# z of jobs 1 to 3 made by VectorE from PSUM in a routed expert layer

## What is computed

```python
expert_ids = jnp.minimum(tid // (25000 // 4), 3)
for e in range(4):
    g = silu(einsum('bsd,fd->bsf', layernorm(x), ctx[e]))
    u = einsum('bsd,fd->bsf', layernorm(x), ctx[e])
    y = einsum('bsf,df->bsd', g * u, ctx[e])
    out = where(expert_ids == e, y, out)
x = x + tanh(g_xattn) * out
x = x + tanh(g_ffn) * fp8_linear(layernorm(x), weight)
```

## Time and profile before

| what | value |
|---|---|
| time, median of 3 runs | 197.42 us (197.24 to 197.56) |
| the profiled execution's own time | 197.25 us |
| its span in the trace | 195.5 us, so 1.75 us lie around it |
| busy: PE, DVE, ACT, POOL | 152.9, 152.7, 112.2, 82.6 us |
| z by POOL (L372) | 3 instructions, 1268 ns mean |
| az by ACT (L654) | 3 instructions, 678 ns mean |
| z by DVE (L892) | 16 instructions, 749 ns mean |

### The profile page before, as it was taken

How to read it: one execution, slowest core, us unless ns; L and a number is a source line. 1 busy time by engine, 2 the same in 40 slices (tenths; PEclk the granted TensorE clock), 3 DMA queues, 4 the chain that set the end, 5 groups by cost and what they waited for, 6 DMA issues and landing times.

```text
span 195.5 us, 3211 instructions
## 1 busy us (share of the span) xinstructions
PE 152.9 (78%) x799; PEld 76.7 (39%) x804; DVE 152.7 (78%) x349; ACT 112.2 (57%) x166; POOL 82.6 (42%) x117
## 2 busy tenths in 40 slices
PE   0141949799999799899999899999977689998300
PEld 0110425244555344444444445554433357673100
DVE  2886799898767799899998898667677699999600
ACT  3355598697443855667788634424413689976400
POOL 8258787412311343324465675111111003488770
PEclk9999999999999999999999999999999999999965
DMA  2837998300000221122212111000000000234451
GB/s 48 329 109 192 367 407 278 103 2 0 0 3 0 55 54 30 33 48 57 55 27 54 30 27 27 3 0 0 2 5 0 0 0 6 105 132 169 184 215 54
DMA packets 15440, 15.68 MB, mean 80 GB/s; under 512 B 10816, under 2 KB 11328, under 8 KB 15424
## 3 DMA queue, kind: packets, MB, share of 16 engines
q1 hardware_dynamic: 12576, 7.09, 12.4%
q0 software_dynamic: 2560, 8.39, 11.8%
q10 hardware_dynamic: 288, 0.00, 0.1%
HBM read 8.92 MB, written 4.19 MB: 67 GB/s over the span
## 4 chain that ended last, share of the span: by engine, by line
DVE 39%; PE 32%; issue 12%; POOL 8%; ACT 4%; DMA 1%; DVEq 1%; POOLq 0%
PE four_ps L465 9%; PE four_ps L457 9%; PE four_ps L474 9%; DVE w_hi L1077 5%; DVE x L1088 5%; POOL x L341 3%; DVE zT_lo L897 3%; PE four_ps L503 3%; DVE bn L863 3%; POOL out L364 3%; DVE bn L911 2%; DVE w_lo L855 2%; DVE hT_hi L1084 2%; DVE x L905 2%; DVE z L892 1%
## 5 line engine op out<-in xcount | busy, mean ns | idle before, releaser
L359 POOL TENSOR_TENSOR rstd<-var,minus_half 128x1 f32<-128x1 f32 x16 | 8.8, 551 | 49.8 <-DVE var L919 49.8
L364 POOL DMA_INDIRECT out<-x,token_of x16 | 19.7, 1231 | 21.0 <-DVE x L1088 17.7
L457 PE MATMUL four_ps<-w_hi,hT_hi 128*128 x76 | 21.3, 391 | 1.4 <-ACT w_hi L624 1.3
L663 ACT ACTIVATE zT_hi<-four_ps 128x512 f16<-128x512 f32 x19 | 11.3, 594 | 18.2 <-PE four_ps L503 18.2
L652 ACT ACTIVATE sg<-four_ps,job_inv_a 128x512 f32<-128x512 f32 x19 | 12.9, 679 | 13.7 <-PE four_ps L474 12.4
L457 PE MATMUL four_ps<-w_hi,zT_hi 128*128 x76 | 19.5, 379 | 1.1 <-DVE x L905 1.1
L341 POOL DMA_INDIRECT x<-in_x,token_of x16 | 17.4, 1087 | 7.1 <-issue 4.2
L643 ACT ACTIVATE w<-x,nmr,rstd 128x512 f32<-128x512 f32 x16 | 13.0, 810 | 12.8 <-DVE nmr L925 12.4
L465 PE MATMUL four_ps<-w_lo,zT_hi 128*128 x76 | 19.5, 379 | 0.0
L465 PE MATMUL four_ps<-w_lo,hT_hi 128*128 x76 | 19.5, 379 | 0.0
L474 PE MATMUL four_ps<-w_hi,zT_lo 128*128 x76 | 19.5, 379 | 0.0
(11 more groups left out here) (146 smaller groups left out, 310.7 us busy)
## 6 DMA issues: line engine op xcount, KB each, us to landing
w<-in_ctx_t SPq DMA_DIRECT2D x4, 1024.0 KB, 9.4
wf<-in_wf_t SPq DMA_DIRECT2D x1, 512.0 KB, 15.4
x<-in_x,token_of POOLq DMA_INDIRECT x16, 6.0
out<-x,token_of POOLq DMA_INDIRECT x16, 2.8
hT_hi<-h_row SPq DMA_TRANSPOSE x9, 2.3
hT_lo<-h_row SPq DMA_TRANSPOSE x9, 2.3
ids_s<-in_ids SPq DMA_DIRECT2D x1, 8.0 KB, 2.7
g_s<-in_g_x ACTq DMA_DIRECT2D x1, 0.5 KB, 2.9
```

What stands on the lines that cost most here:

```text
L364: pool.indirect_dma_start(out, bass.IndirectOffsetOnAxis(ap=token_of[:, i:i + 1], axis=0), block_of(x1, i), None, bounds_check=T - 1).then ...
L457: pe.matmul(ps, lhs_hi(k), w_block(w_hi, expert, k), start=(k == 0), stop=False)
```

## The change

`z_on_pool` goes. POOL no longer has a `z_of`, ACT no longer writes `az`, and the block `az` and its semaphore go with them. DVE's `z_of(j)` now runs in every job, at the place that it already had in jobs 4 to 18: behind `var_first`, which in jobs 1 and 2 is ahead of `w_scaling(j+1)`.

```diff
-        az = sb("az", [P, D], F32)
...
-        def z_on_pool(j):
-
-            return 0 < j < E
...
-            def z_of(j):
-
-                pool.wait_ge(silu_done, j + 1)
-                pool.wait_ge(az_done, j)
-                pool.wait_ge(zT_done, j)
-                pool.tensor_tensor(z[:, :], az[:, :], sg[:, :], ALU.mult).then_inc(z_done, 1)
-
             def job(j):
-                if z_on_pool(j):
-                    z_of(j)
...
                 act.activation(sg[:, :], a_ps[:, :], ACT.Silu, scale=job_inv_a[:, bass.ds(j, 1)]).then_inc(silu_done, 1)
-                if z_on_pool(j):
-                    act.activation(az[:, :], a_ps[:, :], ACT.Copy, scale=job_z_mul[:, bass.ds(j, 1)])\
-                        .then_inc(az_done, 1)
...
-                if fixed and j < JOBS and not z_on_pool(j):
+                if j < JOBS:
                     z_of(j)
```

More of the change, by code:

```diff
@@ L201, in gated_experts_kernel @@
         hT_hi_done, hT_lo_done = sem("hT_hi_done"), sem("hT_lo_done")
-        a_done, az_done, silu_done, z_done, zT_done = sem("a_done"), sem("az_done"), sem("silu_done"), sem("z_done"), sem("zT_done")
+        a_done, silu_done, z_done, zT_done = sem("a_done"), sem("silu_done"), sem("z_done"), sem("zT_done")
         zT_hi_done, zT_lo_done, y_done, x1_done = sem("zT_hi_done"), sem("zT_lo_done"), sem("y_done"), sem("x1_done")
```

## The result

| what | before | after |
|---|---|---|
| time, median on the same chip | 197.33 us (197.22 to 198.11) | 197.87 us (197.78 to 198.21) |
| ratio to before | 1 | 1.0028, 95% interval 1.0014 to 1.0041 |
| the profiled execution | 197.25 us | 197.91 us |
| its span, and what lies around it | 195.5 + 1.75 us | 195.9 + 2.01 us |
| busy: PE, DVE, ACT, POOL | 152.9, 152.7, 112.2, 82.6 us | 153.9, 153.6, 110.7, 79.0 us |

The change costs 0.54 us (197.87 - 197.33), a little beyond the 0.2% that a measurement of this kernel can tell. I had forecast +0.26.

A forecast was written before the change was run, and what follows sets the result against it. DVE was taken as scarce in jobs 1 and 2, PE in job 3. The sum +0.69 - 0.90 + 0.69 - 0.22 + 0 = +0.26 us gave 197.51 to 197.68, forecast 197.6, range 197.1 to 198.2.

The forecast's parts named there:

- `w_bits` is freed: DVE, jobs 1 and 2: without POOL's z, w_bits falls from 1.13 and 0.45 us to 0.23.
- Jobs 1 and 2: DVE's added z less the freed w_bits: job 1 gains 0.21 us, and at job 2's end the shift is +0.26.
- The 0.69 for a z: Cost of one z on DVE between var and row_sq: 0.69 us, bounded by 0.66 and 0.77.
- Job 3: Third z costs nothing, covered by DVE's idle time before add_y with 0.27 us to spare; uncovered, up to 0.69.
- rival 3: Job 2: DVE waits for sg in front of z, w_scaling(3) queued behind; 197.5 to 198.1; chance 0.04.
- Rivals 1, 2 and 4: 1: w_bits stays long, +1.38, chance 0.08; 2: third z uncovered, up to +0.95, 0.04; 4: second z hidden, -0.43, 0.08.
- From job 3 on PE is never idle: Claim that everything after job 3 is released by PE and moves along with the +0.26 us.
- the removed work: ACT's three az and POOL's three instructions: dropping them gains nothing beyond the freed w_bits.
- I see nothing after job 3 that could give it back or add to it: After job 3 to the kernel's end: the +0.26 us shift stays unchanged.
- "the same" (0.65): Chance 0.65 that the time stays within what a measurement can tell from no change, about 0.2% or 0.39 us.
- The test that I named: Sign of a wrong forecast: a different shift after 60 us than at 50.
- The rule that spoke against the change: Trainium skill: offloading saturated DVE may pay, though GpSimd might not help; its first half implies rival 1's time, 198.63.

The follow-up runs named there:

- e5: Kernel before, POOL's z kept, with w_bits of jobs 1 and 2 written by four one-column DVE instructions with one SBUF input each; 196.30 us, 0.9946.
- e7: Changed kernel plus unneeded POOL fills of a dead block beside w_bits in jobs 1 and 2, and two fills at POOL's start; 198.55 us.
- e8_filled: Changed kernel with az and its semaphore back, plus one-column ACT copies and POOL fills with three waits in jobs 1 to 3; 197.45 us, 1.0008.
- e6_pool_reads: Changed kernel plus an unneeded POOL product of two SBUF blocks beside w_bits in jobs 1 and 2, and two fills at POOL's start; 200.12 us.
- e4_z_behind: Changed kernel with DVE's z behind w_scaling instead of ahead of it in jobs 1 and 2; 196.29 us, 0.9947.

## Why the prediction was right in its steps and short in its sum

- *`w_bits` is freed.* Right: 0.22 us in every job. That POOL's product had held it, argued from ends within 0.05 us, is shown by e5 to e7.
- *Jobs 1 and 2.* Right to 0.02 us: -0.21 and then +0.25 in after (forecast -0.21 and +0.26), -0.24 and +0.22 in e8_filled, and 0.45 for job 2 alone (forecast 0.47). The 0.69 for a z, taken from the seam behind `var` in a later job, held: 0.67 in both jobs. With the stand-ins the whole kernel came out where the sum has it: +0.24 at equal clock in e8_filled, forecast +0.26.
- *Job 3.* Right: 0.28 us to spare, forecast 0.27, and no gap on PE.
- *No wait for `sg`* (rival 3). No idle time stands before z in jobs 1 to 3 of after. The mechanism is real, though: in e6_pool_reads, where the granted clock from 30 to 34 us was 0.57, DVE idled 0.36 us before z of job 1 until `sg` came.
- *Rivals 1, 2 and 4* didn't come: `w_bits` wasn't long, the third z was covered, the second wasn't hidden.
- *A misreading without a price.* "From job 3 on PE is never idle" goes beyond its rows, which end at 59 us: from 150 to 160 us PE is busy 6.25 of 10.00 us. The shift was carried through such places all the same, 0.35 us at 53 us and at the last store.
- *The step that failed* is the one on the removed work and the one that added the sum to the profiled execution. I wrote that POOL's gain "is only what it no longer does to `w_bits`" and set 197.25 + 0.26, with the 1.75 us around the span unchanged; "I see nothing after job 3 that could give it back or add to it" was wrong there. POOL's shorter program cost 0.28 us (2.02 - 1.74, means of all executions). With it the sum is 0.26 + 0.28 = +0.54. That the medians differ by just that is in part chance: at equal clock it is 0.60, and 0.09 of the profiled difference is the scatter ahead of the jobs. The 0.28 took the time, at 197.87 inside the range (197.1 to 198.2), over the line from "the same" (0.65) to "slower" (0.28). The test that I named, a shift that stays the same after 60 us, held within the span and couldn't see it.
- *The rule that spoke against the change* (the Trainium skill, Perfetto Trace Analysis, "Optimizing Scalar/DVE Operations") says that moving work off a full DVE may pay, and that to GpSimd it might not help. Both halves are seen here. With z ahead of `row_sq` the offload to GpSimd was the cheaper way by 0.26 us: it cost 0.90 + 0.22 us of hold on the chain, against 2 x 0.69. With z behind `w_scaling` DVE does it for nothing, and the offload costs its whole hold.

The change took 1.12 us of hold off the chain and put 2 x 0.69 us of work into it, in the one place where it counts. The gain was there, as e4_z_behind shows, one step further down the queue.

## What to carry to other kernels

When two engines end within hundredths of a microsecond of each other, ask whether the shorter instruction was held, and what inputs both read; a hold goes away with one input less as well as with the work taken elsewhere (-0.90 us here, with the work left where it was). When work moves to a busy engine, look for that engine's own idle time behind its next release, not for the place where the code already has it: 0.86 us before `w_lo` hid a z that cost 0.69 us ahead of `row_sq`. And look at the time around the span as well: the shorter program of POOL was paid for there with 0.28 us.

## What the runs showed of the hardware that I had not expected

- Taking three instructions and their waits off POOL made the kernel 0.28 us slower outside the span, and three fills of one column (0.10 to 0.12 us each) gave it back. The lone packet on "q14 instruction" moved from 185.6 us to 197.2.
- Taking one of the three off moved it to 193.4 to 194.2 us, and the span ended 0.35 us later with the last store unmoved.
- Four DVE instructions of one column with one input took 0.34 us together, where one of four columns with two inputs takes 0.23 us free and 0.45 to 1.13 us beside POOL's product.
